# Moving two fp32 low-part subtractions from VectorE to GpSimd in a layernorm, attention and gated-FFN kernel

## The chip, the cores and the metric

One core of one Trainium2 chip runs the kernel. The metric is the device time of one execution in microseconds (us). The core has five instruction streams that this text names: TensorE (PE, with its weight loader PEld), VectorE (DVE), ScalarE (ACT), GpSimd (POOL) and SyncE (SP), which only issues DMAs here.

## The reference

There are 16 batches of 512 tokens with 256 features. Each batch is normalised, and the normalised x feeds both a causal attention with 16 heads of 16 features and a gated FFN with 768 hidden features and integer weights scaled by 1/127.

```python
xn = _layernorm(x)                       # x: 16 x 512 x 256, float32
s  = attention(xn, Wq, Wk, Wv, Wo)       # 16 heads, causal softmax
g  = silu(ffn(xn))                       # (silu(xn Wg') * (xn Wu')) Wd'
x  = x + s * g
```

## The kernel before

**Two parts for one fp32 value.** Projections and FFN products are done in a fast 32-bit matmul format that keeps fewer bits. So an operand is split: `hi` is the value copied by ScalarE into that format, and `lo` is the value minus `hi`. A product is then a sum of two or three matmuls (`parts_product`, line 194): hi by hi, and hi by lo each way. Each low part is one subtraction that needs the finished `hi`, and the matmuls wait for the low part.

**Units and tables.** The work of a batch is cut into units, and tables written out by hand (`HEAD`, `PERIOD`, `TAIL`) give one order for them. `PERIOD` runs 13 times, for b = 1 to 13; each pass carries the attention of one batch and prepares the next ones. In a table "qk 2 0 2" is unit `qk`, batch b + 2, index 0, PSUM bank 2. Every engine walks the same table in the same order and does its own share of each unit, so a table also fixes the order of each engine's queue. Engines meet through one semaphore for each kind of result (`after` waits, `signal` or `then_inc` raises).

**The units that matter here.**

- `lb` (POOL, lines 266 and 268): subtracts the mean from, and multiplies by rstd, the transposed x, two instructions on 128 partitions x 1024.
- `lx` (lines 275 and 279): ACT copies the normalised x to `xt_hi`, once all products of the previous batch that read it are done; then a subtraction gives `xt_lo`, 128 x 1024. This is 15 times in a run: twice in `HEAD`, 13 times in `PERIOD`. Batch 0 has its own path.
- `qk`, `v`, `gg`, `gu`: the products that read `xt_hi` and `xt_lo`. The first one, `qk` with index 0, waits for both.
- `st` and `pv`: scores on PE, exponentials on ACT (line 500), the causal selects on POOL (line 507), then the product with v (line 525).
- `on` (POOL, line 566) divides the attention's output by its sums, after the DMAs of `od` and `ob`; `os` (lines 573 and 576) splits it into `o_hi` on ACT and `o_lo`, 128 x 512, 32 times in a run. `op` is the output product, which waits for both halves of `o_lo`; `od` reads the next half into the same buffer, so its DMA on SP waits for `o_lo` too.
- `hs` (POOL, line 393): the low part of the FFN's hidden values, `h_lo`, six times a batch; `dn` is the product that reads it. `mt` (line 463) transposes row maxima.
- `sm`, `mk` and DVE's row maxima (line 457) belong to the softmax.

In `PERIOD` the order around the first change is this (line 88 and 89 of the table):

```
st 1 9 45, ob 0 1, gg 1 5 6, lx 2 0, gu 1 4 0, gu 1 5 3,
dn 1 0 1, hs 1 3, mt 1 1 5, qk 2 0 2, on 0 1, hs 1 4, ...
```

PE's share of that stretch is `gu` 4 and 5 of the old batch, then `dn`, then `mt`, then `qk` of the new batch. The copy in `lx` can start only after `gu` 5.

Of the kernel before, what the change touches and what calls it, by code (L numbers as in the profile page):

```python
# [47 lines left out]
def table(text):  # L48
# [53 lines left out]
    dn 1 0 0, on 0 1, pv 1 4, ob 0 1, pv 1 5, st 1 10 34, st 1 11 56, gg 1 3 1, os 0 1, st 1 12 34, st 1 13 56, pv 1 6,  # L102
    od 1 0, or 1 0, st 1 14 01, st 1 15 34, gu 1 3 2, st 1 16 56, st 1 17 01, pv 1 7, st 1 18 34, pv 1 8, ob 1 0, op 0 0 6,
    st 1 19 34, on 1 0, pv 1 9, pv 1 10, pv 1 11, od 1 1, op 0 1 0, os 1 0, hs 1 3, gg 1 4 2, gu 1 4 3, or 1 1, gg 1 5 3,
    hs 1 4, ob 1 1, gu 1 5 0, hs 1 5, zr 0 0, os 1 1, xr 1 0, zr 1 0, on 1 1, dn 1 1 6, op 1 0 1, op 1 1 4""")
BRANCH = [kind for kind, *_ in HEAD].index("if")


def build(nc, x, xT, wqT, wkT, wvT, woT, wgT, wuT, wdT, out, scratch_o, scratch_r, scratch_m):
    with ExitStack() as ctx:  # L110
# [59 lines left out]
        def r(ap):  # L170
            return ap.bitcast(F32R)
# [13 lines left out]
        def after(e, name, beta, k):  # L185
            wait(e, sems[name], nth(name, beta, k))

        def signal(ins, name):
            ins.then_inc(sems[name], 1)
# [80 lines left out]
        def u_lx(en, e, beta, par, k, banks, prev):  # L270
            if en == "act":
                after(e, "d_xn", beta, 0)
                for name, last in (("f_qk", 3), ("f_v", 1), ("f_gg", FT - 1), ("f_gu", FT - 1)):
                    after(e, name, beta - 1, last)
                e.activation(r(XT[0][:]).rearrange("p k s -> p (k s)"), XTR[:].rearrange("p k s -> p (k s)"), ACT.Copy)\
                 .then_inc(sems["d_xh"], 2)
            elif en == "dve":
                after(e, "d_xh", beta, 1)
                e.tensor_tensor(r(XT[1][:]), XTR[:], XT[0][:], ALU.subtract).then_inc(sems["d_xl"], 2)  # L279

# [287 lines left out]
        def u_os(en, e, beta, par, k, banks, prev):  # L568
            if en == "act":
                if k == 0:  # L570
                    after(e, "f_op", beta - 1, 1)
                after(e, "d_on", beta, k)
                signal(e.activation(r(OT[0][:, k, :]), OC[:], ACT.Copy), "d_oh")
            elif en == "dve":
                after(e, "d_oh", beta, k)
                signal(e.tensor_tensor(r(OT[1][:, k, :]), OC[:], OT[0][:, k, :], ALU.subtract), "d_ol")

# [98 lines left out]
        def u_fl(en, e, beta, par, k, banks, prev):  # L676
# [6 lines left out]
            elif en == "dve":  # L683
# [3 lines left out]
                e.tensor_scalar(FLAG[:], LOW1[:], 0.0, None, ALU.is_le).then_inc(s_flag, 1)  # L687

        UNIT = dict(gm=u_gm, rw=u_rw, wt=u_wt, ld=u_ld, xr=u_xr, la=u_la, lm=u_lm, lc=u_lc, lt=u_lt, lb=u_lb, lx=u_lx, tr=u_tr, qk=u_qk, ls=u_ls, v=u_v, gg=u_gg, gu=u_gu, hs=u_hs,
                    fl=u_fl, dn=u_dn, sm=u_sm, mk=u_mk, mt=u_mt, zr=u_zr, st=u_st, pv=u_pv, od=u_od, ob=u_ob, on=u_on, os=u_os, op=u_op)  # L690
        UNIT["or"], UNIT["if"] = u_or, u_if

# [144 lines left out]
```

## Time and profile before

| What | Value |
|---|---|
| median of 3 runs | 945.88 us (945.82 to 946.13) |
| the profiled execution's own time | 947.55 us |
| its span, first to last instruction | 945.8 us |
| mean granted TensorE clock | 0.998 |
| PE busy | 914.8 us (97%) |
| DVE busy | 707.2 us (75%), 950 instructions |
| ACT busy | 585.8 us (62%) |
| POOL busy | 495.1 us (52%), 681 instructions |

Busy time counts from the start of an instruction to its end; matmuls are pipelined and their ends are modelled, so a PE that shows 97% is not proved to be at its peak. An engine's idle time before an instruction is put down to the engine whose result ended the wait. A row of a timeline gives the start in us, the duration in us, the engine, the line, the operation, output and inputs with shapes and the count of merged instructions; in brackets stands the idle time before it and what ended it. "issue" is a wait for nothing that the profile shows.

### The profile page before, as it was taken

How to read it: one execution, taken by the hardware profiler on the slowest of the kernel's cores; microseconds unless marked ns; L12 is line 12 of the kernel's file. 1: busy time of each engine (PE TensorE's matmuls, PEld its weight loads, DVE VectorE, ACT ScalarE, POOL GpSimd, SP SyncE). 2: the span in 40 equal slices, each digit the busy share in tenths (PEclk: the TensorE clock that was granted, in tenths of full speed). 3: DMA queues.
4: the chain of work that ended last, by engine and by line, in shares of the span. 5: the costliest groups of instructions: out<-in, count | busy, mean ns of one | idle time of the engine just before them, and what ended most of it. 6: DMA issues, size and time to landing. Idle time of an engine off the chain costs nothing.

```text
span 945.8 us, 22760 instructions
## 1 busy us (share of the span) xinstructions
PE 914.8 (97%) x9065; PEld 685.6 (72%) x9065; DVE 707.2 (75%) x950; ACT 585.8 (62%) x796; POOL 495.1 (52%) x681
## 2 busy tenths in 40 slices
PE   3999999999999999999999999999999999999995
PEld 2777767776868777686877868777786867768654
DVE  5985868778696887868788786877778697776823
ACT  5356664757576675756657575665757557575771
POOL 4253553736456464645636455473745547364553
PEclk9999999999999999999999999999999999999999
DMA  6704235353353534535343453534345253543323
GB/s 221 213 25 170 84 116 169 100 198 132 134 164 127 170 106 179 154 125 171 129 151 126 170 152 117 176 132 158 130 148 162 104 185 120 175 131 135 118 93 98
DMA packets 84507, 133.97 MB, mean 142 GB/s; under 512 B 13680, under 2 KB 34928, under 8 KB 84336
## 3 DMA queue, kind: packets, MB, share of 16 engines
q1 hardware_dynamic: 84400, 132.47, 41.8%
q8 instruction: 75, 1.23, 0.5%
q14 instruction: 32, 0.26, 0.1%
HBM read 53.22 MB, written 25.75 MB: 83 GB/s over the span
## 4 chain that ended last, share of the span: by engine, by line
PE 91%; DVE 2%; DMA 2%; POOL 2%; issue 1%; ACT 1%; SPq 0%; POOLq 0%; ACTq 0%; DVEq 0%
PE bank L194 48%; PE values L525 15%; PE bank L434 12%; PE bank L492 11%; PE bank L447 4%; DMA o_reciprocals<-scratch_r 1%; ACT probs L500 1%; DVE row_max L457 1%; PE bank L463 1%; POOL o_compact L566 1%; PE bank L668 0%; DMA scratch_r<-sum_reciprocals 0%; DVE x_in L259 0%; DVE xt_lo L279 0%; DMA sums<-scratch_o 0%
## 5 line engine op out<-in xcount | busy, mean ns | idle before, releaser
L457 DVE TENSOR_REDUCE row_max<-bank 128x2 f32<-128x768 f32 (+3 forms) x352 | 384.9, 1124 | 63.5 <-PE bank L447 60.3
L500 ACT ACTIVATE probs<-bank 128x1024 f32<-128x1024 f32 x320 | 320.4, 1026 | 122.2 <-PE bank L492 120.8
L507 POOL TENSOR_SCALAR_AFFINE_SELECT probs<-probs 128x256 f32<-128x256 f32 (+1 forms) x448 | 194.0, 450 | 275.1 <-ACT probs L500 274.1
L525 PE MATMUL values<-probs,v 128*17 128x512 f32 (+3 forms) x2048 | 166.2, 436 | 0.9 <-POOL probs L507 0.9
L393 POOL TENSOR_TENSOR h_lo<-gated,h_hi 128x512 fp32r<-128x512 f32 x96 | 124.6, 1298 | 74.8 <-ACT h_hi L390 72.7
L434 PE MATMUL bank<-k_stack,q_stack 64*128 64x128 f32 (+3 forms) x1024 | 155.3, 363 | 1.5 <-DVE row_max L457 1.2
L492 PE MATMUL bank<-q_stack,k_stack 64*128 64x512 f32 (+3 forms) x1024 | 142.2, 350 | 1.3 <-DVE row_max L457 0.7
L434 PEld LDWEIGHTS bank<-k_stack,q_stack 64*128 64x128 f32 x1024 | 83.1, 186 | 66.9 <-issue 30.4
L492 PEld LDWEIGHTS bank<-q_stack,k_stack 64*128 64x128 f32 x1024 | 82.9, 186 | 39.1 <-issue 17.3
L366 DVE SCALAR_TENSOR_TENSOR gated<-gated,bank 128x512 f32<-128x512 f32 x96 | 65.8, 685 | 55.4 <-ACT gated L363 55.4
L194 PE MATMUL bank<-xt_hi,wg_hi 128*128 128x256 f32 x384 | 99.3, 293 | 1.6 <-DVE gated L379 1.6
L194 PE MATMUL bank<-wd_hi,h_hi 128*128 128x256 f32 x384 | 93.7, 284 | 3.3 <-POOL h_lo L393 3.3
L194 PE MATMUL bank<-xt_hi,wu_hi 128*128 128x256 f32 x384 | 96.0, 286 | 0.0
L194 PE MATMUL bank<-xt_lo,wg_hi 128*128 128x256 f32 x384 | 94.0, 279 | 0.0
L194 PE MATMUL bank<-xt_lo,wu_hi 128*128 128x256 f32 x384 | 93.2, 279 | 0.0
L194 PE MATMUL bank<-wd_hi,h_lo 128*128 128x256 f32 x384 | 93.0, 282 | 0.0
L447 PE MATMUL bank<-causal_mask,mask_rows_bf 64*128 64x64 bf16 (+2 forms) x1408 | 84.6, 207 | 0.6 <-issue 0.6
L308 ACT ACTIVATE qk_hi<-bank 128x512 fp32r<-128x512 f32 x64 | 38.3, 598 | 74.6 <-PE bank L194 71.1
L525 PEld LDWEIGHTS values<-probs,v 128*17 128x17 f32 x2048 | 44.6, 96 | 47.6 <-issue 39.8
L194 PEld LDWEIGHTS bank<-xt_hi,wg_hi 128*128 128x128 f32 x384 | 73.3, 191 | 6.6 <-DVE gated L379 1.8
L194 PEld LDWEIGHTS bank<-wd_hi,h_hi 128*128 128x128 f32 x384 | 73.2, 191 | 4.5 <-POOL h_lo L393 3.5
L363 ACT ACTIVATE gated<-bank 128x512 f32<-128x512 f32 x96 | 57.6, 600 | 28.9 <-PE bank L194 28.4
(123 smaller groups left out, 1624.4 us busy)
## 6 DMA issues: line engine op xcount, KB each, us to landing
k_stack<-qk_hi SPq DMA_DIRECT2D x64, 256.0 KB, 2.5
q_stack<-qk_hi SPq DMA_DIRECT2D x64, 256.0 KB, 2.5
scratch_o<-o SPq DMA_DIRECT2D x64, 256.0 KB, 2.2
x_again<-x SPq DMA_DIRECT2D x16, 512.0 KB, 4.7
k_stack<-qk_lo SPq DMA_DIRECT2D x32, 256.0 KB, 2.5
q_stack<-qk_lo SPq DMA_DIRECT2D x32, 256.0 KB, 2.6
o_compact<-scratch_o SPq DMA_DIRECT2D x32, 256.0 KB
o_reciprocals<-scratch_r SPq DMA_DIRECT2D x32, 256.0 KB
```

The costliest lines, as they stand in the source:

```text
L194: last = nc.tensor.matmul(dst, r(lhs[a]), r(rhs[b]), start=start and j == 0, stop=stop and j == len(parts) - 1)
L308: signal(e.activation(r(QKP[0][:, k % 2, :]), PS[:, banks[0], :], ACT.Copy), "d_qh")
L363: signal(e.activation(T[:, slot, :], PS[:, banks[0], :], ACT.Tanh, scale=0.5 * SCALE_W), "d_t")
L366: signal(e.scalar_tensor_tensor(out=T[:, slot, :], in0=T[:, slot, :], scalar=1.0, in1=PS[:, banks[0], :], op0=ALU.add, op1=ALU.mult), "d_a")
L393: signal(e.tensor_tensor(r(HT[1][:, f:f + 2, :]).rearrange("p f s -> p (f s)"), T[:, slot, :], HT[0][:, f:f + 2, :].rearrange("p f s -> p ...
L434: nc.tensor.matmul(PS[:, n, j * keys:(j + 1) * keys], r(QS[par][low:low + STACK, pair, i * P:(i + 1) * P]), r(KS[par][low:low + STACK, pai ...
L447: last = nc.tensor.matmul(scores[:, :, i * P + 64 * right:i * P + 64 * right + 64], PICK[low:low + 64, right, :], MASK[low:low + 64, 0:n, ...
L457: signal(e.tensor_reduce(rows, scores, axis=AX.X, op=ALU.max), "d_sm")
L492: last = nc.tensor.matmul(PS[:, n, at:at + w], r(KS[par][low:low + STACK, pair, j * P:(j + 1) * P]), r(QS[par][low:low + STACK, pair, j * ...
L500: signal(e.activation(PR[:, (SCORES * beta + k) % SLOTS, :, :], both(banks), ACT.Exp, scale=SCALE_S), "d_ex")
L507: last = e.affine_select(out=diag, in_=diag, compare_op=ALU.is_ge, fill=0.0, base=0, pattern=[[0, many], [1, P]], channel_multiplier=-1)
L525: last = nc.tensor.matmul(PVB[32 * c:32 * c + VW, j * P:S], V[par][:, j, 4 * g + c, :], PR[:, (SCORES * beta + 5 * g + kind) % SLOTS, pari ...
```

## The change

The two subtractions are issued by GpSimd and no more by VectorE: `xt_lo` in `lx` and `o_lo` in `os`. Their places in the tables stay, except for one unit of `TAIL`: `os 1 1` now comes after `on 1 1`. Both have a share on POOL now, and POOL takes its share in table order, so the division has to come first; on the other engines the move changes no order.

```diff
-    hs 1 4, ob 1 1, gu 1 5 0, hs 1 5, zr 0 0, os 1 1, xr 1 0, zr 1 0, on 1 1, dn 1 1 6, op 1 0 1, op 1 1 4""")
+    hs 1 4, ob 1 1, gu 1 5 0, hs 1 5, zr 0 0, xr 1 0, zr 1 0, on 1 1, os 1 1, dn 1 1 6, op 1 0 1, op 1 1 4""")
@@ u_lx @@
-            elif en == "dve":
+            elif en == "pool":
                 after(e, "d_xh", beta, 1)
                 e.tensor_tensor(r(XT[1][:]), XTR[:], XT[0][:], ALU.subtract).then_inc(sems["d_xl"], 2)
@@ u_os @@
-            elif en == "dve":
+            elif en == "pool":
                 after(e, "d_oh", beta, k)
                 signal(e.tensor_tensor(r(OT[1][:, k, :]), OC[:], OT[0][:, k, :], ALU.subtract), "d_ol")
```

## Rows read from the trace of the kernel before

**Rows 1.** Busy time by window: stretch, then PE, PEld, DVE, ACT, POOL, clock, DMA

```profile
513.40:569.00 55.60, 55.60 (x563) 41.95 (x563) 42.58 (x60) 35.91 (x50) 30.12 (x42) 1.00 0.44 147
...
928.00:931.20 3.20, 0.00 (x1) 0.00 (x1) 1.04 (x2) 0.77 (x2) 2.53 (x2) 1.00 0.21 73
931.20:935.00 3.80, 3.80 (x19) 3.80 (x20) 0.00 (x0) 0.00 (x0) 0.62 (x1) 0.55 0.67 186
```

**Rows 2.** Groups of instructions by line and shape: busy us, mean ns of one

```profile
L566 POOL TENSOR_TENSOR o_compact<-o_compact,o_reciprocals 128x512 f32<-128x512 f32 x32 | 41.5, 1296 | 28.6 <-DMA o_reciprocals<-scratch_r 28.6
...
L268 POOL TENSOR_TENSOR x_transposed<-x_transposed,mean_and_rstd 128x1024 f32<-128x1024 f32 x15 | 36.6, 2439 | 1.2
...
L576 DVE TENSOR_TENSOR o_lo<-o_compact,o_hi 128x512 fp32r<-128x512 f32 x32 | 23.3, 729 | 10.7 <-ACT o_hi L573 10.6
...
L279 DVE TENSOR_TENSOR xt_lo<-x_transposed,xt_hi 128x1024 fp32r<-128x1024 f32 x15 | 19.7, 1316 | 16.7 <-ACT xt_hi L275 16.7
```

**Rows 3.** Timeline of one period around the first product of the new batch

```profile
515.48 2.06 POOL L507 TENSOR_SCALAR_AFFINE_SELECT probs<-probs 128x256 f32<-128x256 f32 x5
...
516.52 1.06 ACT L275 ACTIVATE xt_hi<-x_transposed 128x1024 fp32r<-128x1024 f32 x1 [0.84 <-PE bank L194]
...
517.68 1.23 DVE L279 TENSOR_TENSOR xt_lo<-x_transposed,xt_hi 128x1024 fp32r<-128x1024 f32 x1 [1.28 <-ACT xt_hi L275]
...
519.41 0.39 PE L194 MATMUL bank<-xt_lo,wk_hi 128*128 128x512 f32 x1
...
520.47 1.30 POOL L393 TENSOR_TENSOR h_lo<-gated,h_hi 128x512 fp32r<-128x512 f32 x1 [2.93 <-ACT h_hi L390]
```

**Rows 4.** Waits by engine over the whole span, and PEld's timeline at two loads

```profile
PEld bank L434 <- DVE row_max L457: 20.8, 33, 0.9
...
543.61 0.19 PEld L434 LDWEIGHTS bank<-k_stack,q_stack 64*128 64x128 f32 x2 [0.85 <-DVE row_max L457]
...
561.47 0.30 PEld L492 LDWEIGHTS bank<-q_stack,k_stack 64*128 64x128 f32 x4 [0.85 <-issue]
```

**Rows 5.** Timeline of POOL behind the division in the same period

```profile
560.55 0.77 POOL L507 TENSOR_SCALAR_AFFINE_SELECT probs<-probs 128x256 f32<-128x256 f32 x2
561.75 0.77 POOL L507 TENSOR_SCALAR_AFFINE_SELECT probs<-probs 128x256 f32<-128x256 f32 x2 [0.43 <-ACT probs L500]
563.17 0.64 POOL L507 TENSOR_SCALAR_AFFINE_SELECT probs<-probs 128x512 f32<-128x512 f32 x1 [0.65 <-ACT probs L500]
564.08 0.41 POOL L507 TENSOR_SCALAR_AFFINE_SELECT probs<-probs 128x256 f32<-128x256 f32 x1 [0.28 <-ACT probs L500]
...
566.22 2.42 POOL L266 TENSOR_TENSOR x_transposed<-x_transposed,mean_and_rstd 128x1024 f32<-128x1024 f32 x1
```

**Rows 6.** Timelines of POOL and PE in two late periods, at `lx`

```profile
738.94 2.07 POOL L507 TENSOR_SCALAR_AFFINE_SELECT probs<-probs 128x256 f32<-128x256 f32 x5
...
742.48 0.40 PE L194 MATMUL bank<-xt_lo,wk_hi 128*128 128x512 f32 x1
...
851.46 3.06 POOL L507 TENSOR_SCALAR_AFFINE_SELECT probs<-probs 128x256 f32<-128x256 f32 x5
...
854.53 0.39 PE L194 MATMUL bank<-xt_lo,wk_hi 128*128 128x512 f32 x1
```

**Rows 7.** Timelines of POOL, DVE and PE at the second `lx` of HEAD

```profile
117.75 1.30 POOL L566 TENSOR_TENSOR o_compact<-o_compact,o_reciprocals 128x512 f32<-128x512 f32 x1
...
117.95 2.17 DVE L279 TENSOR_TENSOR xt_lo<-x_transposed,xt_hi 128x1024 fp32r<-128x1024 f32 x1
...
120.52 0.40 PE L194 MATMUL bank<-xt_lo,wk_hi 128*128 128x512 f32 x1
```

**Rows 8.** Timelines of POOL, SP and PE in the tail

```profile
923.25 1.82 POOL L622 TENSOR_TENSOR x_again<-gates,x_again 128x512 f32<-128x512 f32 x1 [0.75 <-DVE gates L615]
...
924.02 0.59 SPq L545 DMA_DIRECT2D sums<-scratch_o  x1
...
937.10 0.38 PE L194 MATMUL bank<-wo_hi,o_hi 128*128 128x256 f32 x1 [1.28 <-DVE o_lo L576]
```

## The prediction, on record before the change was run

> **What bounds the kernel now.** I read the page first. PE is busy for 97% of the span and carries 91% of the chain that ended last. The other engines have room on average: DVE 75%, POOL 52%. The change moves work from the second busiest engine to the least busy one, so averages would call it harmless or good. They can't decide it: what counts is whether PE waits for one of the two results, and whether it waits for DVE today.
>
> The windows view answers the second question for the repeated part. In one period PE is busy for 55.60 of 55.60 us at the full clock [rows 1]. But its ends are modelled, so I looked for waits hidden behind them. The view of waits has PE's weight loader waiting for DVE's row maxima for 20.8 us at one of its lines [rows 4]. The reader is to compare the two loads shown there. Both follow an equal group of eight products with v; before one the loader waits for row_max for 0.85 us, before the other it waits for nothing that is shown, also for 0.85 us [rows 4]. So that time is PE working through the eight, and the row maxima are in time. In the steady periods PE waits for nothing, and each microsecond that it is made to wait is added to the time.
>
> Then I went to the timeline around each result. `o_lo` of both halves is read by `op`, microseconds later. `xt_lo` is the tight one. ACT copies `xt_hi` from 516.52 to 517.58, DVE subtracts from 517.68 to 518.91, and PE's second matmul of `qk` starts at 519.41, 0.50 us behind the subtraction's end [rows 3]. What is the least that this can be? At the second `lx` of HEAD the subtraction ends at 120.12 and that matmul starts at 120.52 [rows 7]; there PE did wait. So 0.40 us is the floor, and the steady period has 0.10 us to spare. The cover is `dn` and `mt`, which PE does between `gu` 5 and `qk`, and it is used up.
>
> **Part 1: `xt_lo` on POOL, 15 times.** DVE is freed of 19.7 us in all [rows 2]. That is worth nothing on the path, since PE doesn't wait for DVE in the periods (above). POOL's time for this shape isn't in the trace. Near it are POOL's multiplication of two operands on 128x1024, 2.44 us, and its 128x512, 1.30 us, which doubled is 2.59 us [rows 2]. I take 2.44, the same size, and keep 2.59 as the upper end; nothing suggests less than 2.4. On DVE it took 1.23 undisturbed [rows 3].
>
> When can POOL start? It finishes five selects at 517.54, just before ACT's result is there at 517.68 [rows 3]. So it starts when DVE did, and ends at 517.68 + 2.44 = 520.12. PE's second matmul comes at 520.12 + 0.40 = 520.52 in place of 519.41: 1.11 us a period. Behind it on POOL is `h_lo`, which begins at 520.47 for ACT's sake anyway [rows 3], so nothing queued there gets later. Everything else in the period hangs on PE and moves along.
>
> Two late periods differ. In one, POOL's selects end only at 738.94 + 2.07 = 741.01, so the matmul comes at 741.01 + 2.44 + 0.40 = 743.85 in place of 742.48, 1.37 us [rows 6]. In the other they take 3.06 us in place of 2.06, which overlaps DVE's subtraction; without that they end at 851.46 + 2.06 = 853.52, and the matmul moves from 854.53 to 856.36, 1.83 us [rows 6]. The 13 periods make 11 x 1.11 + 1.37 + 1.83 = 15.4 us. At the second `lx` of HEAD POOL is in `on` until 119.05 [rows 7]: 119.05 + 2.84 = 121.89 for 120.52, 1.4 us. The first has more work of PE as cover; its cost lies between nothing and the 1.11 of a period, and I take 0.3.
>
> **A rule weighed.** The 2.17 us of DVE's subtraction at 117.95 stand out against 1.23: it began while POOL's division ran until 119.05 [rows 7], and 120.12 less 119.05 is about the undisturbed time. The Trainium skill, "SBUF — State Buffer", section "🔬 SBUF: two separate sides", says why: a VectorE instruction with two SBUF inputs and a GpSimd one that reads SBUF exclude each other for the whole instruction. By that rule the change ends these collisions, since both subtractions leave VectorE. The trace agrees that they exist, but in the steady period shown none touches `xt_lo`, so by this rule too the sum keeps its 1.11 a period.
>
> The Trainium skill, "GPSIMD Engine Reference", section "3.1 Elementwise — side-by-side cycle accounting", gives 4497 ns for 2048 elements of a two-input operation. Halved, an estimate of 2.25 us, it would take 0.19 off each of the 15 and end about 3 us lower. The case's own row of 2.44 stands.
>
> **Part 2: `o_lo` on POOL, 32 times.** POOL takes 1.30 us where DVE took 0.73 on average [rows 2]. In a period the first one stands behind the selects that end at 561.32. POOL then does it until 562.62, the selects of 561.75 until 563.39, those of 563.17 until 564.03, and the next one starts at 564.08 as before [rows 5]: the idle gaps of 0.43 and 0.65 us (and part of 0.28) swallow it, with 0.05 us left. So the two long instructions of `lb` still start at 566.22, and POOL is still free for `xt_lo` in time. The products with v that wait for the delayed selects run after them. The second one falls into POOL's pause before the next scores. In SP's queue the DMAs of `od` wait for `o_lo`; in the periods the reciprocal that needs their data is reached by DVE later. I put all this at nothing; if the gaps weren't there, 1.3 us a period would come back in front of `xt_lo` (the third rival).
>
> **Part 3: the tail.** With the last batch nothing covers the chain division, `o_hi`, `o_lo`, DMA, and so on to the last product. `os 1 0` stands behind the final addition of `op 0 1` in POOL's order, which starts at 923.25 [rows 8]. Undisturbed it takes 1.30 us, then `o_lo` 1.30 with 0.05 between: 925.90, and `od`'s DMA goes out about 925.97 in place of 924.02 [rows 8], 1.95 us late. The last `o_lo`, in front of PE's last product, costs 1.30 for 0.69, 0.6 us more; the unit that moved only keeps it behind its division. Together 2.6 us.
>
> One more term is the clock. After 3.2 us with PE idle the granted clock is down: 0.55 on average in the next window, so mostly the lower level of 1.2 GHz, with 19 matmuls in 3.80 us, 0.20 each [rows 1]. Before its last product PE was idle for 1.28 us [rows 8]; with the 2.6, less what `dn` before it slips, that becomes about 3. That is nearer to the 3.2, so I count the drop: the 12 matmuls of the first half product at 0.10 more each, 1.2 us. Its other end is nothing.
>
> **The sum.** 15.4 + 1.4 + 0.3 + 2.6 + 1.2 = 20.9 us. The profiled execution took 947.55 us, 1.75 more than its span of 945.8; it would take 968.4. The median of the runs is 1.67 lower than it: 945.88 + 20.9, about 966.7 us.
>
> **Rivals.**
>
> - *DVE's relief pays (faster).* If the loader's waits for row_max were PE's own, the 20.8 us of them [rows 4] could vanish with about 43 us less work on DVE, and the periods would gain more than `xt_lo` costs: 966.7 - 20.8 = 945.9 and, with the same waits at the other score matmuls, below it, some 935. It decides from the point where the waits that are real exceed 1.5 us a period. Against it stand the equal 0.85 us and PE's 55.60 of 55.60. Chance 0.05.
> - *The wait is taken back in part.* PE's pause gives ACT, DVE and the DMAs 1.1 us of head start each period; if PE later makes up half of it, the periods cost 7.7: 959. For it speaks little, since PE has no wait there to save. Chance 0.09.
> - *POOL becomes late.* The 0.05 us left behind the first `o_lo` [rows 5] is thin. If POOL falls behind there and brings its full 1.3 us to `xt_lo`, 13 periods cost up to 16.9 more: up to 983, or 975 if half does. Chance 0.10.
> - *The subtraction stays hidden.* POOL would have to take no more than 1.33 us for it (1.23 + 0.10). Then only the tail counts: 948 to 950. The 2.44 of the same shape speaks against it. Chance 0.02.
> - *The forecast.* Chance 0.74, own range 965 (no drop of the clock, first `lx` free) to 970 (2.59 us for each of 15, first `lx` 1.1).
>
> **The numbers.** 0.2% is 1.9 us, about what a measurement of this kernel can tell from no change. Faster has 0.04, the same 0.02, slower 0.94; the first rival's milder end lies within 0.2%. The range must hold 8 in 10: the forecast, most of the second rival and the mild end of the third, 959 to 972.
>
> **What the profile after would show.** Right: `xt_lo` on POOL at 2.4 us; PE idle about 1.1 us before `qk` in each period, released by POOL; the period 56.7 us in place of 55.6; the selects and `lb` in their old places against PE; DVE's busy time down by about 43 us with no gain on PE. The tail's `od` leaves 2 us later against the last scores. Wrong: a period still of 55.6 us; PE idle but shorter than 0.9; `lb` later than before; or PE's idle time in front of the score matmuls gone.

## The result, and the profile after

The changed kernel takes 967.13 us (median of 4 runs, 965.00 to 969.22) where the kernel before takes 945.89 (4 runs, 945.82 to 946.13). The ratio is 1.0215, with a 95% interval of 1.0197 to 1.0233. The forecast was 966.7.

The first look is at the groups of the two instructions that moved, and at the waits behind them. Groups by line and shape (busy us, mean ns), after:

```profile
L576 POOL TENSOR_TENSOR o_lo<-o_compact,o_hi 128x512 fp32r<-128x512 f32 x32 | 41.2, 1288 | 27.1 <-ACT o_hi L573 27.1
...
L279 POOL TENSOR_TENSOR xt_lo<-x_transposed,xt_hi 128x1024 fp32r<-128x1024 f32 x15 | 36.0, 2402 | 3.3 <-ACT xt_hi L275 3.1
```

Waits over the span (us in total, times, longest), after:

```profile
PEld bank L434 <- DVE row_max L457: 20.8, 33, 0.9
...
PE bank L194 <- POOL xt_lo L279: 15.3, 15, 1.9
...
POOL x_transposed L266 <- DMA mean_and_rstd<-scratch_m: 3.4, 5, 1.2
```

GpSimd takes 2.40 us for `xt_lo` and 1.29 for `o_lo`. The wait of PE for `xt_lo` is new, 15 times. The loader's 20.8 us of waits for the row maxima, on which the rival that forecast a gain rested [rows 4], are there to the digit, although DVE now does 43 us less. That time is PE's own work, as the equal 0.85 us had said.

A usual period, on the timeline of all engines, after; it answers to [rows 3]:

```profile
580.90 2.06 POOL L507 TENSOR_SCALAR_AFFINE_SELECT probs<-probs 128x256 f32<-128x256 f32 x5
...
581.95 1.06 ACT L275 ACTIVATE xt_hi<-x_transposed 128x1024 fp32r<-128x1024 f32 x1 [0.84 <-PE bank L194]
...
583.16 2.40 POOL L279 TENSOR_TENSOR xt_lo<-x_transposed,xt_hi 128x1024 fp32r<-128x1024 f32 x1 [0.19 <-ACT xt_hi L275]
...
584.50 0.27 PE L463 MATMUL bank<-identity,row_max 128*128 128x128 f32 x1
585.62 0.50 PE L194 MATMUL bank<-xt_hi,wk_hi 128*128 128x512 f32 x1 [0.84 <-POOL xt_lo L279]
585.95 0.40 PE L194 MATMUL bank<-xt_lo,wk_hi 128*128 128x512 f32 x1
```

Read it as the prediction did. The selects end at 582.96, `xt_hi` is there at 583.01, GpSimd starts at 583.16 and ends at 585.56; PE's transpose stood at 584.50 and the second matmul of `qk` comes at 585.95, 0.39 behind the subtraction. The row shows 0.84 us of idle time only, because it counts from the modelled end of the transpose. From start to start the transpose and `qk` are 1.12 us apart; they were 0.03 apart in the usual period before.

Busy time by window, one such period from transpose to transpose (PE, PEld, DVE, ACT, POOL, clock), after; it answers to the first of [rows 1]:

```profile
413.00:469.70 56.70, 55.85 (x564) 41.96 (x563) 41.23 (x55) 35.74 (x49) 35.06 (x45) 1.00 0.43 144
```

PE has 0.85 us of idle time, and the clock stays at its full level through pauses of this length.

GpSimd behind the division, where the first `o_lo` of a period stands; it answers to [rows 5]:

```profile
570.26 0.78 POOL L507 TENSOR_SCALAR_AFFINE_SELECT probs<-probs 128x256 f32<-128x256 f32 x2
571.00 1.29 POOL L576 TENSOR_TENSOR o_lo<-o_compact,o_hi 128x512 fp32r<-128x512 f32 x1
572.24 1.35 POOL L507 TENSOR_SCALAR_AFFINE_SELECT probs<-probs 128x256 f32<-128x256 f32 x3
573.87 0.41 POOL L507 TENSOR_SCALAR_AFFINE_SELECT probs<-probs 128x256 f32<-128x256 f32 x1 [0.28 <-ACT probs L500]
...
576.01 2.42 POOL L266 TENSOR_TENSOR x_transposed<-x_transposed,mean_and_rstd 128x1024 f32<-128x1024 f32 x1
```

The three selects behind `o_lo` run without a gap, the next one waits for ACT again, and `lb` starts 5.75 us behind the first of these rows; before it was 5.67. The gaps swallowed the 1.29 us, as forecast.

Not every period is like this. Here the wait is longer, after:

```profile
519.54 2.42 POOL L266 TENSOR_TENSOR x_transposed<-x_transposed,mean_and_rstd 128x1024 f32<-128x1024 f32 x1 [1.23 <-DMA mean_and_rstd<-scratch_m]
...
524.43 2.07 POOL L507 TENSOR_SCALAR_AFFINE_SELECT probs<-probs 128x256 f32<-128x256 f32 x5
...
524.56 1.06 ACT L275 ACTIVATE xt_hi<-x_transposed 128x1024 fp32r<-128x1024 f32 x1 [1.22 <-POOL x_transposed L268]
...
526.47 2.37 POOL L279 TENSOR_TENSOR xt_lo<-x_transposed,xt_hi 128x1024 fp32r<-128x1024 f32 x1
...
526.74 0.27 PE L463 MATMUL bank<-identity,row_max 128*128 128x128 f32 x1
...
528.89 0.50 PE L194 MATMUL bank<-xt_hi,wk_hi 128*128 128x512 f32 x1 [1.89 <-POOL xt_lo L279]
```

GpSimd's `lb` waited 1.23 us for a DMA. The whole queue behind it slipped, and it reached `xt_lo` at 526.47, 0.85 us after `xt_hi` was ready (524.56 + 1.06 = 525.62). From transpose to `qk` it is 2.15 us: PE lost 2.1 us and not 1.1.

**Where the 20.4 us between the two spans are** (966.2 and 945.8), worked out from the starts of the same PE instructions in both timelines:

| Stretch | before | after | change | forecast |
|---|---|---|---|---|
| start to the first transposes | 13.99 | 12.85 | -1.1 | 0 |
| to the first matmul of the second `qk` group | 106.19 | 107.82 | +1.6 | 1.7 |
| 13 periods | 734.04 | 751.03 | +17.0 | 15.4 |
| from there to the end | 91.62 | 94.53 | +2.9 | 3.8 |

"13 periods" runs from the second `qk` group of `HEAD` to the one of the last period; it also holds the end of `HEAD`, and a period by itself takes about 55.8 us before. Traces of one and the same kernel differ in the first and the last row. The kernel before has a second trace (experiments 9 and 10), with 11.58 us to the first transposes, 734.07 for the periods and 92.75 for the rest. So the middle rows carry the result, and 1 to 2 us in the outer ones are within what an unchanged kernel shows.

### The profile page after: what moved, and what is told of

Its sections match the earlier page's. It is cut to its first block, busy times and chain, and to the rows that moved or that the text cites. A ratio compares the mean times of both kernels' runs of the same rounds, so it can differ in the third digit from the quotient of the medians.

```text
span 966.2 us, 22760 instructions
## 1 busy us (share of the span) xinstructions
PE 919.6 (95%) x9065; PEld 688.4 (71%) x9065; DVE 664.4 (69%) x903; ACT 585.1 (61%) x796; POOL 565.0 (58%) x728
## 3 DMA queue, kind: packets, MB, share of 16 engines
q8 instruction: 75, 1.23, 0.5%
## 4 chain that ended last, share of the span: by engine, by line
PE 73%; POOL 12%; DMA 7%; DVE 3%; issue 2%; ACT 2%; SPq 1%; POOLq 0%; ACTq 0%; DVEq 0%
PE bank L194 39%; PE values L525 12%; PE bank L434 10%; PE bank L492 8%; POOL xt_lo L279 4%; PE bank L447 3%; DMA o_reciprocals<-scratch_r 2%; DMA mean_and_rstd<-scratch_m 2%; POOL probs L507 2%; POOL x_transposed L268 2%; POOL x_transposed L266 2%; DMA scratch_m<-mv 1%; DVE row_max L457 1%; ACT probs L500 1%; ACT xt_hi L275 1%
## 5 line engine op out<-in xcount | busy, mean ns | idle before, releaser
L507 POOL TENSOR_SCALAR_AFFINE_SELECT probs<-probs 128x256 f32<-128x256 f32 (+1 forms) x448 | 188.8, 440 | 215.9 <-ACT probs L500 214.9
L311 DVE TENSOR_TENSOR qk_lo<-bank,qk_hi 128x512 fp32r<-128x512 f32 x64 | 44.2, 691 | 50.4 <-ACT qk_hi L308 50.4
```

The source lines that it names most:

```text
L311: signal(e.tensor_tensor(r(QKP[1][:, k % 2, :]), PS[:, banks[0], :], QKP[0][:, k % 2, :], ALU.subtract), "d_ql")
L507: last = e.affine_select(out=diag, in_=diag, compare_op=ALU.is_ge, fill=0.0, base=0, pattern=[[0, many], [1, P]], channel_multiplier=-1)
```

## The experiments

The kernel before was run beside each group on the same chip. Its median there was 947.46 us for experiments 1 to 4 (945.22 to 949.37), 945.49 for 5 to 8 and 947.76 for 9 to 11. So ratios, or differences from that median, are what can be compared. Most expectations were counted from 945.9, and in experiments 1 to 4 and 9 to 11 the kernel before alone is 1.6 to 1.9 us above that.

**1. Only `xt_lo` on GpSimd.**

```diff
 def u_lx:
-            elif en == "dve":
+            elif en == "pool":
```

> Only xt_lo moves to GpSimd; o_lo stays on VectorE and TAIL is as before. Theory (PE's cover in front of the first qk is used up, and the late periods come from a DMA): the periods cost what they cost in the changed kernel, 17 us, the start-up about 0.5, and the 2.9 us of the tail are gone: about 964. Rival (GpSimd comes late to xt_lo because it also carries o_lo in the same stretch): with 1.3 us a period less on GpSimd, no period costs more than 1.12 us: 945.9 + 13 x 1.12 + 0.5 = 961. Rival (DVE's relief pays): below 950.

Measured: 965.81 us, ratio 1.0179 (1.0154 to 1.0203). That is 18.4 us over the kernel before where 18 were expected, and most of the 1.0215: this edit carries the loss. Its 13 periods take 750.3 us, 16.3 more than before, and its longest waits at `qk` (1.64 to 1.78 us from start to start) are there without `o_lo` on GpSimd. The rival with a GpSimd made late by `o_lo` falls. Waits in this kernel:

```profile
PE bank L194 <- POOL xt_lo L279: 15.0, 15, 1.5
...
POOL x_transposed L266 <- DMA mean_and_rstd<-scratch_m: 3.5, 6, 0.9
```

The second row is much the same as in the changed kernel, 3.4 us there: it is the DMA in front of `lb` that makes some periods worse.

**2. Only `o_lo` on GpSimd**, with the unit moved in `TAIL`.

```diff
 def u_os:
-            elif en == "dve":
+            elif en == "pool":
```

> Only o_lo moves to GpSimd, with the move in TAIL; xt_lo stays on VectorE. Theory: the periods take 55.6 us as before, since the two o_lo lie in gaps of GpSimd; only the tail grows, by 1.9 us at os 1 0, 0.4 to 0.6 at os 1 1 and up to 0.6 by the clock: 948.2 to 948.8. Rival (o_lo pushes GpSimd's chain lb, selects back and xt_hi and the selects with it): PE waits in the periods and the time is over 950. Rival (DVE's relief pays): under 945.5.

Measured: 948.50 us, ratio 1.0009 (0.9998 to 1.0019), 1.0 us more and not clear of nothing. Expected were 2.3 to 2.9 over 945.9; that 948.50 lies in the range named is owed to this chip's higher times. The tail did grow. From the same group of eight products with v, one of the last, to the end it lasts 48.7 us, and 45.2 and 46.4 in the two traces of the kernel before. But the 13 periods take 733.4 us where those have 734.0 and 734.1. So part of the tail's cost may be paid back in the periods, which no theory here had.

**3. The subtraction twice on VectorE.** Nothing moves to GpSimd; `xt_lo` is only later. The line that makes the semaphore `s_twice` is left out here.

```diff
             elif en == "dve":
                 after(e, "d_xh", beta, 1)
+                e.tensor_tensor(r(XT[1][:]), XTR[:], XT[0][:], ALU.subtract).then_inc(s_twice, 1)
+                e.wait_ge(s_twice, beta)
                 e.tensor_tensor(r(XT[1][:]), XTR[:], XT[0][:], ALU.subtract).then_inc(sems["d_xl"], 2)
```

> The kernel before, with xt_lo's subtraction done twice in a row on VectorE, the second waiting for the first; the result is the same. Theory (what costs is how late xt_lo is, on whatever engine): the second ends at 517.68 + 1.23 + about 0.1 + 1.2 = 520.2 in the period shown, PE waits 1.1 to 1.2 us there, 13 times, and 1 us or so in the start-up: about 961. The periods are alike, since no queue of GpSimd stands between, and the runs agree within 0.5 us. Rival (what costs is GpSimd as the place: its queue, or collisions with VectorE): within 3 us of 945.9.

Measured: 965.26 us, ratio 1.0184 (1.0167 to 1.0202), the same as with `xt_lo` on GpSimd. Timeline of a usual period of this kernel:

```profile
354.52 1.23 DVE L279 TENSOR_TENSOR xt_lo<-x_transposed,xt_hi 128x1024 fp32r<-128x1024 f32 x1 [1.22 <-ACT xt_hi L275]
355.85 1.23 DVE L281 TENSOR_TENSOR xt_lo<-x_transposed,xt_hi 128x1024 fp32r<-128x1024 f32 x1
...
355.98 0.27 PE L465 MATMUL bank<-identity,row_max 128*128 128x128 f32 x1
357.13 0.50 PE L194 MATMUL bank<-xt_hi,wk_hi 128*128 128x512 f32 x1 [0.89 <-DVE xt_lo L281]
```

From transpose to `qk` 1.15 us, the expected 1.1 to 1.2. What costs is the 1.2 us that the low part is late, not the engine that makes it. The expected time was 961, though, 15 us over the kernel before, and 17.8 were measured. The periods were not alike: five of the 13 waits are between 1.29 and 1.89 us. In all five `lb` had waited for its DMA. Timelines of POOL and DVE in one of them, in this kernel:

```profile
518.59 2.42 POOL L266 TENSOR_TENSOR x_transposed<-x_transposed,mean_and_rstd 128x1024 f32<-128x1024 f32 x1 [0.68 <-DMA mean_and_rstd<-scratch_m]
...
523.50 2.08 POOL L509 TENSOR_SCALAR_AFFINE_SELECT probs<-probs 128x256 f32<-128x256 f32 x5
...
524.92 1.73 DVE L279 TENSOR_TENSOR xt_lo<-x_transposed,xt_hi 128x1024 fp32r<-128x1024 f32 x1 [1.22 <-ACT xt_hi L275]
```

Only in the longest of the five was `xt_hi` itself late. In the other four it came on time, but the selects behind the late `lb` still ran when VectorE began, and its subtractions were stretched: here to 1.73 us, ending 1.07 behind the selects, as in [rows 7]. So a late landing costs time even with nothing moved to GpSimd.

**4. More cover, taken from elsewhere.** The changed kernel with one unit of `PERIOD` moved:

```diff
-    ... mk 1 21 01, pv 1 3, st 1 8 23, ...
-    dn 1 0 1, hs 1 3, mt 1 1 5, qk 2 0 2, ...
+    ... mk 1 21 01, st 1 8 23, ...
+    dn 1 0 1, pv 1 3, hs 1 3, mt 1 1 5, qk 2 0 2, ...
```

> The changed kernel, with pv 1 3 (four products with v, 0.98 us on PE, no other engine has a share) moved in PERIOD from in front of st 1 8 to behind dn 1 0, where PE waits for xt_lo. Theory: the wait shrinks by 0.98 a period, 12.7 us in all: about 954.4. Rival (the wait at qk only shows a delay that sits on another engine and comes back at the next product): no gain, 965 to 967.

Measured: 966.62 us, ratio 1.0190 (1.0165 to 1.0216): my expectation of 954.4 was wrong. The wait for `xt_lo` mostly went, from 15.3 us to 3.5. Waits of this kernel, then its timelines of DVE and PE at the old place of `pv 1 3`:

```profile
PE bank L492 <- DVE row_max L457: 9.1, 14, 0.7
...
PE bank L194 <- POOL xt_lo L279: 3.5, 5, 1.4
```

```profile
573.08 4.81 DVE L457 TENSOR_REDUCE row_max<-bank 128x2 f32<-128x1024 f32 x4
...
576.81 0.79 PE L492 MATMUL bank<-q_stack,k_stack 64*128 64x128 f32 x8 [0.65 <-DVE row_max L457]
```

In its old place the unit covered VectorE's row maxima. Four of them run there back to back, 4.81 us, and PE's next scores need a bank that they release. In the kernel before, the weight loader's row at that place shows only the kind of wait that [rows 4] has:

```profile
512.59 0.58 PEld L492 LDWEIGHTS bank<-q_stack,k_stack 64*128 64x128 f32 x8 [0.85 <-DVE row_max L457]
```

There PE worked through the unit's eight matmuls meanwhile, and lost nothing.

**5. The same move in the kernel before**, to see whether that wait has to do with the change.

```diff
-    ... mk 1 21 01, pv 1 3, st 1 8 23, ...
-    dn 1 0 1, hs 1 3, mt 1 1 5, qk 2 0 2, ...
+    ... mk 1 21 01, st 1 8 23, ...
+    dn 1 0 1, pv 1 3, hs 1 3, mt 1 1 5, qk 2 0 2, ...
```

> The kernel before with pv 1 3 alone moved behind dn 1 0. Theory (pv 1 3 hides a wait for VectorE's row maxima in front of st 1 8, which has nothing to do with the change): PE waits about 0.65 us there in each of 13 periods and gains nothing at qk: 8.5 us over the kernel before. Rival (the wait at st 1 8 in the run of the changed kernel came from GpSimd's lateness): no more than 1 us over it.

Measured: 955.07 us, ratio 1.0101 (1.0085 to 1.0117), 9.6 us more. 8.5 were expected. In its trace PE waits 9.1 us for row_max, 14 times, as in experiment 4 (0.7 us, once, without the move): that wait is not the change's.

**6. Cover in both places.** `gg 1 5` (0.94 us on PE) takes the old place of `pv 1 3`:

```diff
-    ... mk 1 21 01, pv 1 3, st 1 8 23, or 0 1, st 1 9 45, ob 0 1, gg 1 5 6, lx 2 0, ...
-    dn 1 0 1, hs 1 3, mt 1 1 5, ...
+    ... mk 1 21 01, gg 1 5 4, st 1 8 23, or 0 1, st 1 9 56, ob 0 1, lx 2 0, ...
+    dn 1 0 1, pv 1 3, hs 1 3, mt 1 1 5, ...
```

> The changed kernel with pv 1 3 (0.98 us on PE) behind dn 1 0 again, and in its old place gg 1 5 (0.94 us on PE, bank 4; st 1 9 on banks 5 and 6), which before stood in front of lx. So PE has work both while VectorE does its row maxima and while GpSimd does xt_lo. Theory (the time is PE's uncovered wait, wherever it lies): the wait at qk shrinks by 0.98 and nothing opens at st 1 8: 13 x 0.98 = 12.7 us less than the changed kernel, about 954.5. Rival (moving work only moves the wait, as in the run with pv 1 3 moved alone, because VectorE or ACT bounds this stretch anyway): 964 to 967.

Measured: 965.41 us, ratio 1.0205 (1.0180 to 1.0229), wrong again by 11 us. The row_max wait is gone, and this is left:

```profile
PE bank L194 <- POOL xt_lo L279: 7.6, 15, 1.4
```

The usual wait from transpose to `qk` fell from 1.12 to between 0.56 and 0.70, not by 0.98. The reason is in [rows 3]: GpSimd came free only 0.14 us before the subtraction could start. With `gg` 5 earlier, `gu` 5 and `xt_hi` are earlier too, GpSimd isn't, and the cover gained in front is lost behind its queue. Timelines of ACT and POOL in a usual period of this kernel:

```profile
579.83 1.06 ACT L275 ACTIVATE xt_hi<-x_transposed 128x1024 fp32r<-128x1024 f32 x1 [0.47 <-PE bank L194]
...
579.50 2.10 POOL L507 TENSOR_SCALAR_AFFINE_SELECT probs<-probs 128x256 f32<-128x256 f32 x5
581.54 2.42 POOL L279 TENSOR_TENSOR xt_lo<-x_transposed,xt_hi 128x1024 fp32r<-128x1024 f32 x1
```

`xt_hi` is there at 580.89, and GpSimd takes it up 0.65 us later, when its selects are done.

**7. The order of experiment 6 in the kernel before.**

> The kernel before with the same reordering of PERIOD. Theory: in the usual period there is no wait at qk to save, so nothing changes there; what can go is the wait in the periods in which the data of lb land late, 0.3 us each in a few of them: 0 to 1.5 us less than the kernel before on the same chip. Rival (the new order opens a wait on ACT or VectorE): 2 us or more above it.

Measured: 949.87 us, ratio 1.0040 (1.0026 to 1.0054), 4.4 us more where my theory had up to 1.5 less, though no wait of PE in its periods shows it. Its 13 periods take 737.5 us for 734.0, which is 0.27 a period. Beside the trace of before, the groups of products take longer where the kinds of product alternate otherwise: `gg` 5 is followed by the next kind 1.13 us after its start here and 1.06 there, and `gu` 4 and 5 lose 0.16. So this order has a price of its own, and what causes it is not known. It closes the sum of experiment 6: the waits at `qk` are 6.8 us shorter in all than in the changed kernel, the order costs 3.5, and the 13 periods came out 2.9 shorter (748.1 for 751.0).

**8. One half each.** In the kernel before VectorE subtracts one half of `xt_lo`, GpSimd the other.

```diff
-            elif en == "dve":
+            elif en in ("dve", "pool"):
+                k = ("dve", "pool").index(en)
                 after(e, "d_xh", beta, 1)
-                e.tensor_tensor(r(XT[1][:]), XTR[:], XT[0][:], ALU.subtract).then_inc(sems["d_xl"], 2)
+                signal(e.tensor_tensor(r(XT[1][:, k, :]), XTR[:, k, :], XT[0][:, k, :], ALU.subtract), "d_xl")
```

> The kernel before with xt_lo split: VectorE subtracts one half (128x512), GpSimd the other, both as soon as xt_hi is there. Each alone would take 0.7 and 1.3 us. If the two exclude each other on SBUF (the Trainium skill, SBUF - State Buffer, section on the two sides), they run one after the other, 0.6 + 1.3 = 1.9 us, and PE waits about 0.6 us a period: 945.9 + 13 x 0.6 + 1 = 955. If they overlap, the pair ends after 1.3 us and PE waits at most 0.1 to 0.2: 947 to 949.

Measured: 953.83 us, ratio 1.0080 (1.0065 to 1.0096), 8.3 us more where 9 were expected if the two exclude each other. Timelines of POOL, DVE and PE in a usual period of this kernel:

```profile
182.09 1.80 POOL L280 TENSOR_TENSOR xt_lo<-x_transposed,xt_hi 128x512 fp32r<-128x512 f32 x1
...
182.04 0.69 DVE L280 TENSOR_TENSOR xt_lo<-x_transposed,xt_hi 128x512 fp32r<-128x512 f32 x1 [1.21 <-ACT xt_hi L275]
...
183.95 0.50 PE L194 MATMUL bank<-xt_hi,wk_hi 128*128 128x512 f32 x1 [0.18 <-POOL xt_lo L280]
```

GpSimd's half takes 1.80 us and not 1.30, while VectorE's, begun 0.05 before it, takes its usual 0.69: the second waited for the first. The Trainium skill, "SBUF — State Buffer", section "🔬 SBUF: two separate sides", says that of two such instructions the one that starts first keeps the other out for its whole length. The trace agrees roughly: one wholly after the other would be 0.64 + 1.29 = 1.93 us from GpSimd's start, and 1.80 were measured.

**9 and 10. The late periods: does a big DMA hold up the small ones?** The DMA of the transposed x goes out at the start of `PERIOD`, in the kernel before and in the changed one; the kernel before was also run once more for its trace.

```diff
-    ld 2 0, on 0 0, zr 0 0, ob 0 0, pv 0 11, sm 1 16 45, lt 2 0, st 1 1 01, la 2 0, ...
+    ld 2 0, lt 2 0, on 0 0, zr 0 0, ob 0 0, pv 0 11, sm 1 16 45, st 1 1 01, la 2 0, ...
```

> The kernel before once more, unchanged, for its trace on this chip: qk reached with 0.03 us between it and the transpose in front in most periods, and up to 0.3 in a few in which the data of lb land late. Theory: these late periods are the kernel's own and not the change's.

> The kernel before with the DMA of the transposed x (lt, 512 KB) issued at the start of PERIOD, behind ld, and not 3 us ahead of the two small DMAs of mean and rstd that lb waits for. Theory (the late periods come from those small DMAs landing behind the big one): they land after 1.4 us each time, and the periods are all alike: 0.3 to 1.5 us less than the kernel before. Rival (their lateness has another cause): no difference, or the x_in data land late and VectorE's statistics with them: slower by up to 2 us.

> The changed kernel with the same earlier DMA. Theory: every period's wait at qk is then 1.11 us and not up to 2.16: 2 to 3 us less than the changed kernel, 964 to 965, with runs that agree within 1 us. Rival (the late periods come from GpSimd's own queue): the waits stay scattered and the time is 966 to 967.

Measured: 946.32 us for the kernel before (one run); 959.43 with the DMA moved, ratio 1.0123 (1.0103 to 1.0142); 981.77 for the changed kernel with it, ratio 1.0362 (1.0342 to 1.0382). The kernel before has late periods of its own: `lb` waits 3.3 us for its DMA here, four times (1.5, twice, in the first trace), and one of them shows 0.36 us at `qk`. The rest of my theory fell: with the big DMA moved, the reciprocals behind it come later. Waits of the kernel before with the DMA moved:

```profile
POOL o_compact L566 <- DMA o_reciprocals<-scratch_r: 46.9, 16, 3.9
...
PE values L525 <- POOL probs L507: 5.6, 10, 1.1
```

GpSimd waits 46.9 us for the reciprocals in place of 28.6 [rows 2], its selects stand behind that, and PE's products with v behind the selects. PE's wait for the selects grew by 4.7 us of the 11.0 that the periods cost; the rest was not traced. Late landings remain in several periods. Timeline of SP in the late period of the changed kernel that is shown above:

```profile
512.62 0.32 SPq L242 DMA_DIRECT2D scratch_m<-mv  x1
515.83 0.32 SPq L248 DMA_DIRECT2D mean_and_rstd<-scratch_m  x1
```

The first of the two stores mean and rstd, 4 KB; the second, which fills 512 KB from it and is not small, goes out once it has landed. That took 1.4 us in most periods, 3.21 here, and 2.1 to 3.2 in four of the changed kernel's five late ones. So the late part is the store's landing. Why it is late stays open.

**11. The addition in front of `o_lo` in the tail.** Only `o_lo` on GpSimd, and in `TAIL`:

```diff
-    ... od 1 1, op 0 1 0, os 1 0, hs 1 3, ...
+    ... od 1 1, os 1 0, op 0 1 0, hs 1 3, ...
```

> Only o_lo on GpSimd, as in the run with o_lo alone, and in TAIL os 1 0 stands ahead of op 0 1, so GpSimd does o_lo before the final addition. Theory (the addition in front of it is what makes it 1.9 us late): the third o_lo ends 0.6 us later than in the kernel before and not 1.9, and of the tail's 2.9 us some 1.5 go: 1 to 1.5 us over the kernel before. Rival (the tail is longer for another reason, such as the clock of its last products): at least 2.5 us over it.

Measured: 947.88 us, ratio 1.0008 (0.9996 to 1.0021), 0.1 us more where 1 to 1.5 were expected. The times can't tell this from experiment 2, the traces can. Timeline of POOL in this kernel:

```profile
918.96 1.29 POOL L566 TENSOR_TENSOR o_compact<-o_compact,o_reciprocals 128x512 f32<-128x512 f32 x1 [1.20 <-DMA o_reciprocals<-scratch_r]
921.05 1.29 POOL L576 TENSOR_TENSOR o_lo<-o_compact,o_hi 128x512 fp32r<-128x512 f32 x1 [0.80 <-ACT o_hi L573]
922.29 1.27 POOL L622 TENSOR_TENSOR x_again<-gates,x_again 128x512 f32<-128x512 f32 x1
```

`o_lo` comes before the addition and ends 24.1 us behind the group of products named in experiment 2; there it was 25.6, and 23.4 in the trace of [rows 8]. The tail lasts 47.5 us for 48.7. So 1.5 us of `o_lo`'s delay was the addition, and the tail got 1.3 shorter where 1.5 was expected.

## Why the prediction was right

**What bounds the kernel: right.** PE's time is the kernel's time, and VectorE's relief didn't shorten any of the waits named. It may not be quite worthless: with `o_lo` alone off VectorE the periods were 0.7 us shorter in sum in experiment 2 and 1.7 in experiment 11. That is 0.05 to 0.13 us a period, and I had put it at nothing. But the two kernels have the same periods and differ by 1.0 between themselves, one trace each, so a gain of this size is not shown. Its cause was not tested either; VectorE's `o_lo` took 0.73 on average and 0.68 undisturbed, which fits collisions with GpSimd, and is only argued.

**`xt_lo`: right in mechanism and size.** The same arithmetic gave 1.11 us a period; the traces show 1.09 (1.12 from transpose to `qk`, less the 0.03 of before). GpSimd's 2.40 us stand for the 2.44 taken from `lb`. The estimate of 2.25 from the Trainium skill, "GPSIMD Engine Reference", section "3.1 Elementwise — side-by-side cycle accounting", is further off than the row. Experiments 1 and 3 tie the loss to this edit, and to lateness alone. The 0.40 us from the subtraction's end to the second matmul held as well, at 0.39.

**The late periods: undersized.** I gave two of the 13 an extra, 1.0 us in sum. After the change five of them exceed 1.12 by 2.6 us in sum. I had read their lateness from one trace of before, in which `lb` waits twice; in its second trace it waits four times, and ACT's 0.84 us of idle time in front of `xt_hi` hides most of that. With no time to spare, each late landing reaches PE. The 4 us over which the runs spread are not explained by this: the kernel before spread over 0.3 on that chip, but over 4.2 on two of the three others.

**`o_lo` in the periods: right.** The gaps took it, with `lb` 0.08 us later. **The start-up: right**, 1.6 for 1.7 (0.4 and 1.2 for the 0.3 and 1.4 of the two `lx`). The 1.1 us given back before it by a faster load aren't the change's: that stretch took 11.6, 12.8 or 13.9 us in the traces kept, 13.99 and 11.58 in the two of the kernel before.

**The tail: right in mechanism, oversized.** `od` left 1.82 us later against PE's last scores (1.95 forecast), and experiment 11 shows that the addition was most of it. The clock is the term that was mis-sized. PE's last product and VectorE's first step on it, after:

```profile
956.88 0.39 PE L194 MATMUL bank<-wo_hi,o_hi 128*128 128x256 f32 x1 [2.25 <-POOL o_lo L576]
...
957.56 0.41 PE L194 MATMUL bank<-wo_hi,o_lo 128*128 128x256 f32 x1
...
959.36 0.69 DVE L615 SCALAR_TENSOR_TENSOR gates<-bank,gates 128x512 f32<-128x512 f32 x1 [2.67 <-PE bank L194]
```

Busy time by window (PE, PEld, DVE, ACT, POOL, clock) there:

```profile
954.00:958.00 4.00, 1.75 (x13) 1.54 (x12) 0.69 (x1) 1.11 (x2) 2.08 (x2) 0.93 0.19 66
958.00:962.00 4.00, 3.48 (x18) 3.27 (x17) 2.03 (x4) 0.00 (x0) 1.29 (x1) 0.63 0.02 4
```

PE had been idle for 2.25 us and not for about 3, since `dn` slipped by 1.3. The first matmuls still ran at the full level, and the granted clock fell while they did (0.93, then 0.63 on average). The other traces agree: with this one, the matmuls of this product slow down in all seven whose wait here was 1.97 to 2.81 us, and in none of the seven where it was 1.57 or less. The length of one pause is not the whole of it, though: with `lt` moved in the changed kernel, PE waited 2.22 us at a `qk` in the middle of the periods, and the clock stayed at 1.00. From the end of `o_lo` to VectorE's step it takes 2.54 us for 1.84 before: 0.7, where 1.2 was forecast. And the whole miss of 0.9 in the tail is less than the 1.1 us by which the tails of the two traces of before differ; in the second, VectorE's third `o_lo` took 1.49 us beside GpSimd's addition, where the first has 0.69.

So the sum of 20.9 was partly luck. It meets the spans' 20.4 and the medians' 21.2 because 1.6 us too little in the periods stood against 0.9 too much in the tail and the 1.1 that the load gave back.

**The rivals.** No large relief, no hidden subtraction, no wait taken back: the periods give nothing of the 1.1 back. A GpSimd made late by `o_lo` was not seen either, outside the tail. Whether some order of this table hides 2.4 us on GpSimd stays open: three orders were tried, none did.

## What to carry to other kernels

An engine at 52% can be the wrong home for a 1.2 us job, and one at 75% the right one: look at the instruction that waits for the result, and measure the spare time in front of it (0.10 us here) before moving anything slower into it. A queue's place matters as much as its duration, both ends of it: here the new engine also came free just 0.14 us before it was needed, so more cover on the waiting side bought about half of what it should. And a unit that seems free to move may be covering another wait: a loader's "wait" that costs nothing where it stands (0.85 us behind the eight matmuls of a unit) turned into 0.65 us of real time when the unit was taken away.

## What was not expected of the hardware

A two-input subtraction on VectorE and one on GpSimd, started 0.05 us apart, ran one after the other in every usual period (1.80 us for 1.30), so splitting a piece of work over the two gave 1.8 us where VectorE alone needs 1.23. And in the tail the granted clock fell after 2.25 us of idle time, in the middle of the product that followed, so that a later start made even the work behind it slower by 0.7 us; a wait of 2.22 us between two busy periods left it at 1.00. A store of 4 KB took 1.4 us until the next DMA could go in most periods and up to 3.2 in others, in the kernel before as well (up to 2.9), and no run here shows why.
